# A graph network layer chain on one core: moving five pieces of work in the order of four engines

## The reference, cut to what matters

```
h = relu(layernorm(x))
for l in 0, 1, 2:                                    # mask = adjacency or diagonal
    scores = leaky(x @ attn_w[l,:d] + (x @ attn_w[l,d:]).T + attn_b[l])
    agg    = softmax(where(mask, scores, -inf)) @ x
    h1     = layernorm(x + agg) * g1[l] + beta1[l]
    x      = layernorm(h1 + gelu(h1 @ W1[l] + b1[l]) @ W2[l] + b2[l]) * g2[l] + beta2[l]
x = input + x
Wh = relu(layernorm(x)) @ W                          # closing layer
out = x + leaky(softmax(where(adj > 0, leaky(Wh a1 + (Wh a2).T), -9e15), axis=1) @ Wh)
```

## Time and profile before

| what | value |
|---|---|
| median of 3 runs | 2035.45 us (2034.87 to 2035.59) |
| time of the profiled execution | 2034.0 us |
| span of the profiled execution | 2032.2 us |
| PE (TensorE matmul) busy | 1862.5 us, 92% |
| DVE (VectorE) busy | 1560.6 us, 77% |
| ACT (ScalarE) busy | 1252.4 us, 62% |
| POOL (GpSimd) busy | 881.7 us, 43% |
| mean granted TensorE clock | 0.988 |

### The profile page before, as it was taken

The page is one execution under the profiler, slowest core; times in us unless marked ns, Lnnn a source line. Parts: engine busy times, 40 slices in busy tenths (PEclk is TensorE's granted clock), DMA queues, the critical chain, the costliest instruction groups (busy, mean ns, idle before and its releaser), DMA issues.

```text
span 2032.2 us, 30833 instructions
## 1 busy us (share of the span) xinstructions
PE 1862.5 (92%) x11009; PEld 1586.9 (78%) x11009; DVE 1560.6 (77%) x4927; ACT 1252.4 (62%) x1948; POOL 881.7 (43%) x703
## 2 busy tenths in 40 slices
PE   3899999999899989999899998999989999999995
PEld 2787777888788878888778887788877888788884
DVE  6678887688777797778877689677887688777755
ACT  2566666666657565675665666756666666666562
POOL 3355453435433444343534354433453435433450
PEclk9899999999999999999999999999999999999998
DMA  4000100011000110001100011000100011000100
GB/s 166 22 32 22 63 11 22 1 42 35 8 22 1 42 43 1 22 1 48 37 1 22 13 36 37 1 22 22 53 12 21 1 42 32 11 11 1 32 1 21
DMA packets 40625, 52.33 MB, mean 26 GB/s; under 512 B 2926, under 2 KB 30872, under 8 KB 40472
## 3 DMA queue, kind: packets, MB, share of 16 engines
q1 hardware_dynamic: 40472, 50.37, 7.8%
HBM read 41.97 MB, written 8.39 MB: 25 GB/s over the span
## 4 chain that ended last, share of the span: by engine, by line
PE 44%; DVE 36%; POOL 8%; ACT 7%; issue 5%; DMA 0%; DVEq 0%; ACTq 0%; POOLq 0%
PE acc L426 12%; PE acc L493 11%; PE ps_u L465 7%; PE acc L530 5%; POOL columns L1263 5%; DVE probs L938 4%; PE acc L512 3%; DVE junk L906 3%; DVE probs L1071 2%; DVE stats L998 2%; DVE probs L1075 2%; PE ps_t L389 2%; DVE stats L852 2%; DVE normed L970 2%; DVE h_lo L977 1%
## 5 line engine op out<-in xcount | busy, mean ns | idle before, releaser
L493 PE MATMUL acc<-w_hi,gelu_hi 128*128 128x256 f32 x1536 | 463.6, 302 | 17.3 <-POOL gelu_lo L1297 17.3
L723 ACT ACTIVATE g_full<-ps_u,vec_all 128x512 f32<-128x512 f32 x384 | 259.5, 689 | 330.7 <-PE ps_u L465 164.4
L1297 POOL TENSOR_TENSOR gelu_lo<-g_full,gelu_hi 128x512 fp32r<-128x512 f32 x240 | 310.1, 1301 | 313.1 <-ACT gelu_hi L731 253.5
L493 PE MATMUL acc<-w_hi,gelu_lo 128*128 128x256 f32 x1536 | 432.6, 282 | 0.0
L493 PE MATMUL acc<-w_lo,gelu_hi 128*128 128x256 f32 x1536 | 431.9, 281 | 0.0
L426 PE MATMUL acc<-x_nat,probs 128*128 128x257 f32 x1536 | 377.7, 394 | 54.3 <-DVE normed L951 27.1
L426 PEld LDWEIGHTS acc<-x_nat,probs 128*128 128x128 f32 x1536 | 279.5, 191 | 149.8 <-ACT probs L698 43.8
L1263 POOL TENSOR_TENSOR columns<-columns 128x4 f32<-128x4 f32 x128 | 135.8, 1061 | 563.9 <-DVE columns L867 563.9
L493 PEld LDWEIGHTS acc<-w_hi,gelu_hi 128*128 128x128 f32 x1536 | 290.9, 189 | 35.2 <-POOL gelu_lo L1297 29.4
L493 PEld LDWEIGHTS acc<-w_lo,gelu_hi 128*128 128x128 f32 x1536 | 291.7, 190 | 6.1
L493 PEld LDWEIGHTS acc<-w_hi,gelu_lo 128*128 128x128 f32 x1536 | 290.3, 189 | 0.0
(11 more groups left out here) (130 smaller groups left out, 3669.3 us busy)
## 6 DMA issues: line engine op xcount, KB each, us to landing
adj_in<-adj_dram SPq DMA_DIRECT2D x64, 256.0 KB, 2.8
x_nat<-x_dram SPq DMA_DIRECT2D x16, 512.0 KB, 5.2
x_res<-x_dram SPq DMA_DIRECT2D x16, 512.0 KB, 4.1
out_dram<-x_res SPq DMA_DIRECT2D x64, 128.0 KB, 1.7
x_res<-L_gnn_W_dram SPq DMA_DIRECT2D x5, 1024.0 KB, 5.2
mask_g<-L_gnn_W_dram SPq DMA_DIRECT2D x1, 1024.0 KB, 11.7
attn_row<-L_gnn_attn_w_dram SPq DMA_DIRECT2D x1, 512.0 KB
g_row<-L_gnn_g_dram SPq DMA_DIRECT2D x1, 384.0 KB
```

Source lines behind the costliest of these rows:

```text
L493: last = pe.matmul(acc[side][c // 2][:, cols:cols + D], h[:, r, tok], w[:, layer, f, :], start=False, stop=(f == FC - 1 and i == 2), skip_ ...
L723: full = act.activation(g_full[:, f % 2, :], ps_u[f % 2][:, :], ACT.Gelu, bias=b1_col[:, layer, f:f + 1])
L1297: pool.tensor_tensor(gelu_lo[:, f % RING, :], g_full[:, f % 2, :], gelu_hi[:, f % RING, :].bitcast(F32), ALU.subtract).then_inc(lo_done[0] ...
```

## The change

No instruction is added or taken away, and SyncE's list (the DMA queue) is the same. What moves, and where:

- **TensorE.** In slots 1 and 3, `down` 2 and then `scores_row` go ahead of all of `final_out`; before, two chunks of `final_out` came first, then `scores_row`, the other two, and `down` 2. In slot 2, `down` 2 goes ahead of `bound_rows`.
- **ScalarE.** Of the four exps of a closing layer, one (not two) comes at the end of slots 0 and 2, and three come in slots 1 and 3 between the halves of `ff_apply`. In slot 0, `low_row` goes ahead of `final_apply`, and the four copies `final_wh` alternate with the four exps. In slot 2, `final_h` goes ahead of `low_row`.
- **VectorE.** In slot 5 the first two sums of `attention_sum` go ahead of `input_stats`. In slots 4 and 5 the masks of chunk 3 go ahead of `attention_norm`. In slots 0, 1, 3 and 5 `gelu_high` goes ahead of `variance`. In slots 1 and 3 both `final_scale` go behind the scores, and in slots 0 and 2 `h_rest` goes one step forward within `final_bounded`.
- **GpSimd.** In slots 0, 1, 3 and 5 `gelu_rest(n, 0)` goes ahead of the inverse root.

```diff
@@ tensor, slot() @@
                 if s.late is not None:
+                    down(n, side, layer, 2)
+                    scores_row(n + 1)
                     final_out(s.late[0], free, (0, 1), n - 1)
-                if s.late is not None:
-                    scores_row(n + 1)
                     final_out(s.late[0], free, (2, 3))
...
-                if soon or early_turn:
+                if soon:
                     bound_rows(n + 1)
-                down(n, side, layer, 2)
+                if s.late is None:
+                    down(n, side, layer, 2)
+                if early_turn:
+                    bound_rows(n + 1)
@@ scalar, pair_body() @@
                     if s.late is not None:
-                        final_exps(s.late[0], (2, 3))
+                        final_exps(s.late[0], (1, 2, 3))
...
                     if early_turn:
+                        final_h(s.final[0], free)
                         low_row(n + 1)
-                        final_h(s.final[0], free)
                     gelu(n, layer, 4)
                     if s.final is not None and s.layer_a == 0:
+                        low_row(n + 1)
                         final_apply(*s.final)
...
                     if s.final is not None and s.layer_a == 0:
                         final_h(s.final[0], free)
-                        final_wh(s.final[0], free)
-                    exps(n + 1)
+                        for c in range(NC):
+                            final_wh(s.final[0], free, (c,))
+                            exps(n + 1, (c,))
+                    else:
+                        exps(n + 1)
...
-                        final_exps(s.final[0], (0, 1))
+                        final_exps(s.final[0], (0,))
@@ vector, attention_sum(): sum_of(c) is L949 and L951 of one chunk @@
+                if statistics is not None:
+                    sum_of(0)
+                    sum_of(1)
+                    input_stats(*statistics)
+                for c in range(NC):
+                    if statistics is None or c >= 2:
+                        sum_of(c)
                     last = dve.bn_stats(stats[:, c, :], normed[:, c, :])
...
-                    if prepare is not None and c == 0:
+                    if prepare is not None and c == (0 if statistics is None else 2):
                         input_shift(prepare)
@@ vector, ff_norm() @@
+                if follows and (scores is None or late is not None):
+                    gelu_high(n + 1)
                 variance(ln2_chain, n)
-                if follows:
+                if follows and scores is not None and late is None:
                     gelu_high(n + 1)
-                if late is not None:
-                    final_scale(late, 0)
...
-                if late is not None:
-                    final_scale(late, 1)
...
                     dve.wait_ge(s_ready.sem, s_ready.at(step_next))
+                if late is not None:
+                    final_scale(late, 0)
+                    final_scale(late, 1)
@@ vector, final_bounded() @@
                     if j > 0:
                         negate(j - 1)
-                if step is not None:
-                    h_rest(*step)
+                    if step is not None and j == 1:
+                        h_rest(*step)
@@ vector, pair_body() @@
-                        input_stats(s.prepare, s.side, pair + 1)
+                        if s.side == 0:
+                            input_stats(s.prepare, s.side, pair + 1)
...
+                    if s.prepare is not None:
+                        prepare_masks(s.prepare, s.side, (3,))
                     attention_norm(n + 1)
                     if s.prepare is not None:
-                        prepare_masks(s.prepare, s.side, (3,))
                         layer_scores(n + 2, s.side, s.prepare, (n + 1, s.layer_a))
@@ gpsimd, pair_body() @@
+                    low_first = s.begins or s.late is not None or not s.attend or s.layer_a == 0
+                    if low_first:
+                        gelu_rest(n, 0)
                     if not s.begins:
                         inverse_root(ln2_chain, n - 1, ln2_rstd)
-                    gelu_rest(n, 0)
+                    if not low_first:
+                        gelu_rest(n, 0)
```

More of the change, by code:

```diff
@@ L693, in low_row, with exps @@
                 act.activation(low_sb[:, :], ps_t[0][:, :], ACT.Copy).then_inc(low_ready.sem, 1)
-            def exps(n):
-                for j in range(NC):
+            def exps(n, chunks=range(NC)):
+                for j in chunks:
                     act.wait_ge(q_masked[j % 2].sem, q_masked[j % 2].at(n, j // 2 + 1))
@@ L743, in final_h, with final_wh @@
                     act.activation(h_last[:, k, :], banks[k][:, :], ACT.Relu).then_inc(g_act.sem, 1)
-            def final_wh(g, banks):
-                for c in range(NC):
+            def final_wh(g, banks, chunks=range(NC)):
+                for c in chunks:
                     act.wait_ge(wh_done.sem, wh_done.at(g, c + 1))
@@ L815, in pair_body @@
                         final_wh(s.final[0], free)
-                    else:
+                    elif s.final is None:
                         low_row(n + 1)
@@ L942, in bounded_scores, with attention_sum, sum_of @@
                 masked(NC - 1)
-            def attention_sum(n, side, prepare=None, masks=None, graph_normed=None):
-                for c in range(NC):
+            def attention_sum(n, side, prepare=None, masks=None, graph_normed=None, statistics=None):
+                def sum_of(c):
                     dve.wait_ge(agg_done.sem, agg_done.at(n, c + 1))
```

3 lines of the change are left out of this document (2 added, 1 removed).

## The result

The changed kernel takes **2067.02 us** (median of 4 runs, 2062.49 to 2067.98); the kernel before took 2035.16 us beside it. The ratio is 1.0156, 95% interval 1.0137 to 1.0175. The forecast was 2048.8 us: slower, as it said, but by more than twice its figure, and outside its range of 2017 to 2060.

A forecast was written before the change was run, and what follows sets the result against it. The prediction took TensorE, busy 92% of the span, as the bound, so only its waits could be won. Slot terms of +1.9 a pair, seven times +13.3, gave 2047.3, plus 1.45 for the median: 2048.8 us; 80% range 2017 to 2060.

The forecast's parts named there:

- Slots 1 and 3 (+0.7): Slots 1 and 3: `down` 0 wins 1.2, lost again by `down` 1; `attend_out` starts 0.7 later; +0.7 us in each.
- the hold: Slots 1 and 3: GpSimd's low parts keep the shared port, so VectorE's `variance` and then the shift wait, the shift 1.28.
- Slots 2 and 4 (-1.3, -0.7): Slot 2: `down` 2 fills the bound rows' wait, -1.3; slot 4: masks fit into VectorE's wait for the root, -0.7.
- Slot 0 (+1.1): Slot 0: `final_turn` 0.9 late, and a stall of 1.2 within `project` replaces 1.21 behind it; +1.1 us.
- Slot 5 (+1.4): Slot 5: the stall moves from `attend_out` to `turn_tokens`, and bound rows come about 1.6 late; +1.4 us.
- Its two parts: Slot 5: sums ahead of the statistics, -0.3 to +0.3; low part first, making the bound rows about 1.6 late.
- the clock falls: Rival, 7%: new stalls in slot 5 lower TensorE's clock in every pair, 1.0 to 1.7 each; +7 to +12 more, 2058.
- The sum: Slot terms of a steady pair add to +1.9 us, seven times +13.3, on the profiled execution's 2034.0.

The follow-up runs named there:

- L: Low part of gelu 0 ahead of the root; alone on the kernel before 2039.88 us; the changed kernel without it 2027.36 us.
- E: One early final exp, scales behind the scores, `h_rest` early; added to the kernel before with M, D2 and X: 2020.34 us.
- D13: `down` 2 ahead of the final outputs in slots 1 and 3; not run alone.
- M: Mask of chunk 3 ahead of the norm; the kernel before with this and D2 alone: 2019.87 us.
- D2: Bound rows of slot 2 behind `down` 2; the kernel before with this and M alone: 2019.87 us.
- the turn filled: Changed kernel with transposes that compute nothing ahead of `turn_tokens` in slot 5: 2060.53 us with 16, 2045.24 us with 32.
- X: Exps among `wh`'s copies in slot 0; alone on the kernel before: 2030.76 us.
- both waits filled: Changed kernel with 16 transposes that compute nothing ahead of `turn_tokens` and 9 ahead of `bound_rows` in slot 5: 2044.42 us.
- Y: Sums of chunks 0 and 1 ahead of the input statistics; alone on the kernel before: 2038.24 us.
- the better version: Kernel before with M, D2 and X: 2012.75 us; with L in slot 5 alone added: 2005.79 us; with 9 transposes too: 2004.73 us.
- Y and the move: Kernel before with Y and with `residual_shift` of slot 5 moved behind `mask_scores` on GpSimd: 2038.19 us.

## Why the prediction was right in sign and wrong in size

**Slots 1 and 3 (+0.7): right in size, +0.6, but not for the reason given.** The forecast put `down` 1 at 1153.1 in its slot 3, 10.4 into the slot; it started 10.2 into it. It put `attend_out` 0.7 later; it came 0.6 later (28.50 for 27.88). The place of the hold was partly off: only one of the six instructions was held, L870, which took 1.16, while L867 just ahead of it kept its 0.15.

```profile
1166.54 1.31 POOL L1316 TENSOR_TENSOR gelu_lo<-g_full,gelu_hi 128x512 fp32r<-128x512 f32 x1 [7.78 <-DVE gelu_hi L999]
...
1166.72 1.16 DVE L870 TENSOR_SCALAR columns<-columns 128x4 f32<-128x4 f32 x1
...
1168.21 1.01 POOL L1282 TENSOR_TENSOR columns<-columns 128x4 f32<-128x4 f32 x1 [0.36 <-DVE columns L874]
...
1169.55 1.03 DVE L1035 SCALAR_TENSOR_TENSOR columns<-columns 128x2 f32<-128x2 f32 x1
...
1171.23 0.39 PE L493 MATMUL acc<-w_hi,gelu_hi 128*128 128x256 f32 x1 [1.11 <-DVE gelu_lo L1003]
```

The forecast let L and E cancel and charged the 0.7 to D13, the `down` 2 ahead of the final outputs. The runs put it on E: E alone made these slots 44.65 (+0.87), E with D13 44.5, and all parts together 44.4, so next to E D13 is worth -0.1 to -0.2. That the total fits is partly luck.

**Slots 2 and 4 (-1.3, -0.7): right**, and shown alone by the run of M and D2.

**Slot 0 (+1.1): the total is right, by two errors that cancel.** Where no fall came (the runs without L in slot 5 and with the turn filled), slot 0 was 41.85, so that the moves are worth 0.0; the fall adds about 1.4. The waits that the forecast named are there: 1.84 at the turn for 0.68 before, and 1.04 in `project` for the 1.2 forecast:

```profile
1052.58 1.86 PE L435 MATMUL acc<-ident,wh 128*128 128x128 f32 x7 [1.84 <-ACT wh L740]
...
1060.99 1.14 PE L512 MATMUL acc<-w_last,h_last 128*128 128x258 f32 x4 [1.04 <-ACT wh L751]
```

Two terms of the sum were off. `final_turn` was put 0.9 late, and it came 0.6 late (17.24 into the slot for 16.62). And the sum stops at the start of `attend_out`, which came 0.6 late too: it has no term for `attend_out` itself, which takes 6.77 and not 7.31 once its exps are ready, as in the run of X alone. These 0.54 take the 0.6 back. (That TensorE wins at `down` 0 and keeps 0.5 of it changes nothing, since it waits for the turn either way.) The table load takes 1.28 here too, and the exp follows it by 0.01 (1058.65 and 1059.94 in the trace): nothing shows of the drain that the Trainium skill (ScalarE: Activation LUTs, What ACT_TABLE_LOAD costs) adds.

**Slot 5 (+1.4): the step that failed, at +4.7.** The kernel with both waits filled has the change's order without a fall, and there slot 5 is 40.9, 1.6 above the 39.3 of before: the size of the term, with the bound rows 1.5 late for the 1.6 forecast. Its two parts fit less well: Y was put at -0.3 to +0.3, and alone, in the pair without a fall, it costs 1.1, as two instructions of the attention norm's variance are held (1.25 and 1.19) beside GpSimd's `residual_shift`, which the forecast did not see; L then adds 0.5 and not most of 1.4. What the term left out is **3.1 us of slow clock**, two stretches of 3.41 us behind the waits of 2.09 and 3.61. The forecast knew this as the rival "the clock falls" and gave it 7%, with 1.0 to 1.7 a pair. The price of one fall was right for these places: 1.62 in slot 5, 1.08 to 1.6 in slot 0. It is no constant, though: 1.1 in slot 5 of the kernel before, 0.4 to 0.9 in that of the better version with L in slot 5 alone, where a wait of 0.84 behind it takes a part up, and next to nothing with Y alone. The count was wrong: three a pair, not one, because the waits drew one each, that of slot 0 included. The chance was too low: it was read from a wait of 1.94 that drew a fall in pairs 0 and 6 alone, while the forecast's own sums set waits of up to 2.8 in every pair. In these traces, the 2.1 of the bound rows in slot 5 drew a fall in all seven pairs of the changed kernel, in three and four of seven with the turn filled by 16 and by 32, and in one of seven with L alone; the 3.6 drew one in all seven, and the 3.4 of the run with Y alone in six. The Trainium skill (TensorE: Matmul & The Clock Gate, HAM oscillation — how this bites in real kernels) reckons the penalty as half of the slow time, here 1.7 for 3.41. The 1.62 in slot 5 agrees. Slot 0's 1.08 is less, since its stretch begins among the turn's eight transposes, which took 1.72 for 1.58, while the twelve matmuls of `down` 2 behind them took 2.44 for 1.51.

**The sum.** Without falls the slots give 0.0 + 0.6 - 1.3 + 0.6 - 0.6 + 1.6 = +0.9 a pair, about 6 us in seven. The falls give 1.4 + 3.1 = +4.5, less 0.3 for what the kernel before has of its own over its clean 243.9: +5.1 a pair, 30.6 for six, where 29.9 were measured. The forecast had +1.9, so that the gain it missed in slot 0 hid a part of what the clock cost.

**Parts.** L's price of 40 us against 5 alone is found slot by slot: with Y and X and without L, slot 0 is 39.1; L there takes back 2.8 without a fall and 4.2 with one; in slot 5 it takes 2.1 to 2.3 in five of seven pairs, a fall among them. With Y alone, slot 0 was shorter in just the six pairs with a fall at the end of slot 5, and 41.88 in the seventh, so what the fall cost there came back in slot 0. With L in slot 0 it doesn't come back: slot 0 is 41.85 behind a slot 5 that ends in a fall (L in all slots but 5) and behind one that doesn't (turn filled). That the other engines get a start while TensorE is slow, and that L uses it up, fits both, but was not tried. D13 was not run alone; it is in the run without L (44.5) beside E, whose own run gives 44.65.

## What to carry to other kernels

When an order moves a wait of TensorE, add up not only how long it is but whether it may draw a fall of the clock, and whether a later wait takes up what the fall costs: three waits of 1.8 to 3.6 us a pair cost 4.5 us more here than the same order without the falls. To find out, fill the wait with transposes that nobody reads; if the slot gets shorter, the rest of the loss was the clock, and the filling is a remedy of its own. Measure parts together as well as alone: L was worth +5 or +40 us, or -7 in one slot of the best version.

## What the runs showed of the hardware that was not expected

- In the steady part of the 18 traces (slot 5 of pair 0 to slot 3 of pair 7), 104 stretches at 0.50 are 3.41 us long and 11 are 6.83. Those 11 began while TensorE still waited, 0.7 to 1.7 before the wait of 3.4 to 3.6 ended.
- The same wait may draw one or not: the 1.83 in slot 0 did so in all six pairs that have it in the changed kernel, in three of six without L in slot 5, and in four, five and two of six in the three kernels with filled waits (16; 16 and 9; 32 transposes). The 1.94 of the kernel before did in two of seven. Even the 1.29 of slot 0 in pair 2 of the changed kernel drew one, while the 1.4 to 1.5 of slot 2 drew none in 35 cases (the kernel before and those with L, Y, Y and the move, and X).
- GpSimd's instruction slowed too where VectorE was busy beside it: two additions took 3.40 where they take 2.51 elsewhere.
- The single-input L870 (TENSOR_SCALAR, 128x4, float32) was held 1.16 to 1.19, and the mask's conversion from int32 1.49. The Trainium skill (SBUF — State Buffer, Who interferes with whom) lets an instruction with one SBUF input contend when it can enter a two-port mode, and counts `tensor_scalar`, which both are, among those that can. Both agree with that rule; the forecast had used only its part on two inputs.
